# GNN kernel: edge counts summed on GpSimd during the adjacency loop, degrees formed as columns first

## The chip, the cores and the metric

The kernel is one program on one core of a Trainium2 chip. It is written directly for the five engines: TensorE (PE), VectorE (DVE), ScalarE (ACT), GpSimd (POOL) and SyncE (SP). Each engine has its own stream of instructions, and the streams wait for one another on semaphores. The metric is the device time of one execution, in microseconds; lower is better.

## The reference

A graph of 1250 nodes, each with 512 features, and 41250 directed edges, sorted by destination; every node also has its own loop once in the edge list. The work is a chain of four blocks with residual additions. What matters here is the first block, a graph convolution of three layers, and the third, which uses the same graph:

```python
loops = jnp.arange(n, dtype=edge_index.dtype)
src = jnp.concatenate([edge_index[0], loops])
dst = jnp.concatenate([edge_index[1], loops])
deg = jax.ops.segment_sum(jnp.ones_like(dst, dtype=x.dtype), dst, num_segments=n)
dis = jax.lax.rsqrt(jnp.maximum(deg, 1.0))
norm = (dis[src] * dis[dst])[:, None]
for l in range(W.shape[0]):
    h = x @ W[l]
    msg = h[src] * norm
    agg = jax.ops.segment_sum(msg, dst, num_segments=n) + b[l]
    x = jax.nn.relu(agg)
...
cnt = jax.ops.segment_sum(jnp.ones((src.shape[0],), x.dtype), dst, num_segments=n)
mean_agg = agg / jnp.maximum(cnt, 1.0)[:, None]
```

`deg` (edges into a node, plus one) scales the rows before and after each layer; `cnt` (edges into a node) is needed much later, as 1/cnt.

## The kernel before

**The adjacency table.** The kernel turns the edge list into a dense table `CTR`: for each of ten tiles t of 125 source nodes, 125 partitions (the source node in its tile) by 1250 columns (the destination node), holding the number of edges. It is built in 33 batches (`NBAT`) of 1250 edges. For each batch VectorE writes two one-hot tables in f16 (`onehots`, L1536 for the source in its tile, L1541 for source tile and destination slot; each is a TENSOR_TENSOR of two inputs in SBUF), TensorE multiplies them into a PSUM bank (L1052; L1034 opens the bank, L1027 adds the first column of the next batch and so ends the bank), and ScalarE copies 50 columns of all ten tiles into `CTR` (L722) at a place read from a register. ScalarE's copies are counted by the semaphore `placed`. Because edges are sorted by destination, batches fill the table from left to right; columns on the left are final long before the loop ends. Batch b's one-hots go to one of three buffers (`RING`), so VectorE may not start batch b before TensorE has finished batch b-3. In the loop ScalarE also sums rows of X and their squares (L731, L737) for the layer norm; GpSimd has nothing to do from 6.5 us on.

**The stage after the loop.** It is a chain through four engines:

- TensorE waits for all 33 copies (`placed`), then `degrees` (L1083) multiplies a table of ones (`WH`, 128 columns) with all of `CTR`: 3 column splits (500, 500, 250) by 10 tiles, 30 products. The result is the degree of every destination as a row, the same in all 128 partitions, in banks 0 to 2.
- VectorE copies the three pieces into `invc` (L1649, `deg_copied`), then adds the identity to the ten diagonal blocks of `CTR` (`self_loops`, L1644, `loops_ready`).
- TensorE turns the row into columns: ten products of one row of `invc` by a single 1 (L1094, `degcol_ready`), one column per tile, in bank 3.
- ScalarE takes the square root (L743), VectorE the reciprocal (L1653): `dis`. Then for each tile ScalarE writes `YH` = `XHAT`*`dis` rounded (L754) and VectorE the rest `YL` (L1668, `y_ready`), and TensorE starts the first aggregation (L1110: `YH` and `YL` of each tile times `CTR`, 12 groups of 20 products in each of three layers).

`XHAT`, the normalised input, is written by VectorE right behind its last one-hot (L1589, ten TENSOR_SCALARs). Later VectorE takes max(., 1) and the reciprocal of `invc` (L1676, L1677).

The order on every engine is the order in which the code is written; nothing is moved by a scheduler. A flag set during the loop chooses at run time between this path and a slow one for unusual edge lists; with these inputs the first one runs, and the slow path only costs branches. SyncE only starts transfers, of which none is in flight in this stage that anything here waits for.

Of the kernel before, what the change touches and what calls it, by code (L numbers as in the profile page):

```python
# [22 lines left out]
N = 1250  # L23
# [20 lines left out]
FLAG_AT = 5  # L44
SUMS_AT = 2
# [54 lines left out]
def build(nc, a, out):  # L100
    ctx = ExitStack()
    with ctx:
# [3 lines left out]
        def sem(name):  # L106
            return ctx.enter_context(nc.semaphore(name))
# [64 lines left out]
        XT = at("XTF", R_ZH, [128, NT * D])  # L172
        XTH = at("XTH", R_ZH, [128, FT, N], F32R)
# [45 lines left out]
        wbase, edge, offs, holds = carve(NG + 1), carve(NBAT), carve(NG), carve(2 * NG + NBAT)  # L219
# [84 lines left out]
        sp_ready, sp_exp, sp_one, sp_ln = sem("sp_ready"), sem("sp_exp"), sem("sp_one"), sem("sp_ln")  # L304
# [237 lines left out]
        def _(pool):  # L542
# [20 lines left out]

            pool.wait_ge(agg_ready, FT * len(SPLITS) * LAYERS)
# [132 lines left out]
        def _(act):  # L697
# [59 lines left out]
            act.wait_ge(deg_ready, len(SPLITS))  # L757
# [3 lines left out]
            act.wait_ge(sp_one, 1)  # L761
# [242 lines left out]
        def _(pe):  # L1004
# [75 lines left out]
            def degrees(unit, table):  # L1080
                for s, (c0, w) in enumerate(SPLITS):
                    for t in range(NT):
                        mm = nc.tensor.matmul(PS[:, s, 0:w], unit, table[0:NP, t, c0:c0 + w],  # L1083
                                              start=(t == 0), stop=(t == NT - 1))
                    mm.then_inc(deg_ready, 1)

            with pe.If(slow < 1):
                degrees(WH[0:NP, 0, 0:128], CTR)
            with pe.If(slow > 0):
                pe.wait_ge(counts_ready, 1)  # L1090
                degrees(ones[0:NP, :], CT)
# [29 lines left out]
            def gcn(exact):  # L1121
                n_agg = 0
                for l in range(LAYERS):
                    for s, (c0, w) in enumerate(SPLITS):
                        for f in range(FT):
                            if n_agg >= 6:
                                pe.wait_ge(zl_ready, n_agg - 5)
                            tile_wait = None
# [121 lines left out]
            pe.wait_ge(loops_ready, 2)  # L1250
# [219 lines left out]
        def _(dve):  # L1470
# [82 lines left out]
            def check_windows():  # L1553
# [5 lines left out]
                link(v.tensor_scalar(holds[0:1, 2 * NG + NBAT - 1:], wbase[0:1, NG - PER:NG - PER + 1], float(CW - BWIN - 1), None, ALU.is_le))  # L1559
# [35 lines left out]
            with dve.If(slow > 0):  # L1595
                SLOW0, SLOWK = 3, 7
# [597 lines left out]
```

## Time and profile before

| | us |
|---|---|
| median of 3 runs (lowest, highest) | 867.35 (866.24, 869.72) |
| the profiled execution | 867.76 |
| its span, first to last instruction | 865.8 |
| last copy into the table ends | 79.53 |
| the 30 degree products begin, end | 79.70, 88.04 |
| first product of the first aggregation | 93.18 |

| engine | busy us | share of the span |
|---|---|---|
| PE | 794.6 | 92% |
| DVE | 530.7 | 61% |
| ACT | 314.4 | 36% |
| POOL | 140.8 | 16% |

Times in rows are microseconds from the start of the span. "L1083" is line 1083 of the kernel printed above. In a row of a timeline the first number is the start, the second the length of the record; the names after the line are the operation and the tiles it writes and reads. "x30" says that 30 instructions are merged in the row, and brackets tell how long the engine had been idle and who ended that. One f32 product is recorded as two passes; so the ten products of L1094 are twenty records. Records of neighbouring instructions of one engine overlap a little, so the distance between starts is what an instruction costs there.

### The profile page before, as it was taken

The page shows a single profiled execution, that of the slowest core. Times are in us where ns is not written, and L with a number is a line of the kernel's source. Part 1 is how long each engine was busy: PE and PEld are TensorE (multiplying, and loading weights), DVE is VectorE, ACT ScalarE, POOL GpSimd, SP SyncE. Part 2 cuts the span into 40 slices and gives each one's busy share as a digit, 9 for nine tenths or more (in the row PEclk, how much of TensorE's full clock was granted, in tenths as well). Part 3 has the DMA queues.
Part 4 walks back from the last instruction along what each step waited for, and adds up shares of the span by engine and source line. Part 5 has one row for each costly group of instructions (what it writes and reads, how often), then busy time and mean ns, then how long its engine had stood idle before and what let it go on. Part 6 is the DMA issues. An engine that isn't in the chain of part 4 may idle for free.

```text
span 865.8 us, 13538 instructions
## 1 busy us (share of the span) xinstructions
PE 794.6 (92%) x3933; PEld 620.2 (72%) x3934; DVE 530.7 (61%) x949; ACT 314.4 (36%) x522; POOL 140.8 (16%) x186
## 2 busy tenths in 40 slices
PE   3899899999999989997999969987989999999983
PEld 1556788888888876676888847876867777777761
DVE  7777832421431587886024685897477878778751
ACT  1563512511431104533211313332245655556531
POOL 2000000000000300000000500212123443455321
PEclk9999899999999999998999978987989999999997
DMA  7400000000000010000102003002898959874632
GB/s 195 139 2 2 0 1 1 1 1 1 0 1 1 31 51 0 1 1 1 49 1 93 23 1 119 1 0 98 325 350 258 309 90 357 273 192 82 153 62 33
DMA packets 32291, 71.38 MB, mean 82 GB/s; under 512 B 4387, under 2 KB 4637, under 8 KB 32243
## 3 DMA queue, kind: packets, MB, share of 16 engines
q1 hardware_dynamic: 24480, 53.31, 17.7%
q0 software_dynamic: 6272, 14.68, 8.6%
q10 hardware_dynamic: 1491, 2.73, 0.9%
q8 instruction: 32, 0.52, 0.3%
q14 instruction: 16, 0.13, 0.0%
HBM read 96.53 MB, written 12.72 MB: 126 GB/s over the span
## 4 chain that ended last, share of the span: by engine, by line
PE 77%; DVE 15%; issue 3%; ACT 1%; DMA 1%; DVEq 1%; ACTq 0%; POOL 0%; POOLq 0%
PE PS L1110 22%; PE PS L1144 10%; PE PS L1363 9%; PE PS L1410 8%; PE PS L1242 5%; PE PS L1052 4%; PE PS L1357 4%; PE PS L1185 3%; PE PS L1395 3%; PE PS L1034 2%; PE PS L1341 1%; PE PS L1372 1%; PE PS L1083 1%; DVE stats L1892 1%; DVE XN L1480 1%
## 5 line engine op out<-in xcount | busy, mean ns | idle before, releaser
L1110 PE MATMUL PS<-CTR,YH 125*128 125x500 f32 (+1 forms) x480 | 164.1, 357 | 2.3 <-DVE YL L1668 2.3
L1110 PE MATMUL PS<-CTR,YL 125*128 125x500 f32 (+1 forms) x480 | 163.7, 356 | 0.0
L1110 PEld LDWEIGHTS PS<-CTR,YH 125*128 125x128 f32 x480 | 91.5, 191 | 15.5 <-DVE YL L1668 2.6
L1110 PEld LDWEIGHTS PS<-CTR,YL 125*128 125x128 f32 x480 | 91.6, 191 | 13.1
L1986 DVE TENSOR_TENSOR W1L<-WB,W1H 128x1152 fp32r<-128x1152 f32 x56 | 74.0, 1356 | 14.6 <-issue 7.7
L1410 PE MATMUL PS<-WB,YF 128*128 x168 | 78.6, 604 | 2.4 <-issue 1.7
L1695 DVE TENSOR_TENSOR ZL<-PS,ZH 128x500 fp32r<-128x500 f32 (+1 forms) x36 | 21.1, 592 | 90.2 <-ACT ZH L788 90.2
L1363 PE MATMUL PS<-W1H,XGH 128*128 128x384 f32 x168 | 73.5, 438 | 0.0
L961 ACT CAST W1H<-WB 128x1152 fp32r x56 | 64.2, 1151 | 15.9 <-issue 10.9
L1363 PE MATMUL PS<-W1L,XGH 128*128 128x384 f32 x168 | 57.4, 342 | 0.0
L1363 PE MATMUL PS<-W1H,XGL 128*128 128x384 f32 x168 | 56.9, 339 | 0.0
L671 POOL DMA_INDIRECT out<-YF,dest_i x28 | 48.2, 1722 | 34.5 <-ACT YF L936 18.7
L788 ACT CAST ZH<-PS 128x500 fp32r<-128x500 f32 (+1 forms) x36 | 18.1, 508 | 97.3 <-PE PS L1110 97.3
L1410 PEld LDWEIGHTS PS<-WB,YF 128*128 128x128 f32 x168 | 30.4, 194 | 30.8 <-issue 30.8
L1357 PE MATMUL PS<-WB,YF 128*128 x112 | 46.1, 494 | 2.3 <-DVE W1L L1986 2.3
L1144 PE MATMUL PS<-WL,ZH 128*125 128x512 f32 x120 | 47.3, 394 | 0.0
L1144 PE MATMUL PS<-WH,ZH 128*125 128x512 f32 x120 | 47.3, 394 | 0.0
L1144 PE MATMUL PS<-WH,ZL 128*125 128x512 f32 x120 | 47.2, 394 | 0.0
L565 POOL MEMSET FMASK<- 128x1 f32 x1 | 0.1, 99 | 282.6 <-PE PS L1110 282.6
L1052 PE MATMUL PS<-ET 125*128 125x120 f16 x330 | 44.0, 309 | 2.1 <-issue 2.1
L1706 DVE SCALAR_TENSOR_TENSOR tmp<-PS,dis,bias 125x512 f32<-125x512 f32 x30 | 22.5, 751 | 35.7 <-PE PS L1144 35.7
L1052 PEld LDWEIGHTS PS<-ET 125*128 125x128 f16 x330 | 30.4, 135 | 18.3 <-issue 17.4
(386 smaller groups left out, 1638.3 us busy)
## 6 DMA issues: line engine op xcount, KB each, us to landing
WB<-in_w SPq DMA_DIRECT2D x28, 1536.0 KB
WB<-in_w SPq DMA_DIRECT2D x28, 768.0 KB
WB<-in_b SPq DMA_DIRECT2D x28, 384.0 KB
X<-in_x SPq DMA_DIRECT2D x1, 2240.0 KB
xn_dram<-XN SPq DMA_DIRECT2D x1, 2240.0 KB
WNEXT<-in_W SPq DMA_DIRECT2D x2, 1024.0 KB, 9.7
SR<-in_sw SPq DMA_DIRECT2D x1, 1536.0 KB, 7.8
out<-X ACTq DMA_DIRECT2D x1, 1120.0 KB
```

The costliest lines, as they stand in the source:

```text
L671: pool.indirect_dma_start(out[:, :], bass.IndirectOffsetOnAxis(dest_i[:, k:k + 1], 0), yo[:, k, :], None, compute_op=ALU.add).then_inc(sca ...
L961: nc.scalar.copy(W1H[k][:, :, cols], raw[:, :, cols]).then_inc(w1_hi, 1)
L1052: mm = nc.tensor.matmul(windows(b)[:, :, place], oh_lo[b % RING][0:CHUNK, j, :, x], oh_key[b % RING][0:CHUNK, j, :, x].rearrange("p (t w) ...
L1110: mm = nc.tensor.matmul(dest, lhs, rhs, start=(t == 0 and h == 0), stop=(t == NT - 1 and h == 1))
L1144: mm = nc.tensor.matmul(PS[0:NP, 6 + n % 2, :], z[:, f, t * NP:(t + 1) * NP], w[:, f, :], start=(f == 0 and h == 0), stop=(f == FT - 1 and ...
L1185: mm = nc.tensor.matmul(PS[0:TILE[j], 3 + j, 0:RC], w[rows, k, cols], x, start=(k == tiles[0] and h == 0), stop=(k == 2 and h == 2))
L1242: mm = nc.tensor.matmul(PS[:, 4 + n % 4, 0:w], wt[:, f, fo * 128:(fo + 1) * 128], z[:, f, c0:c0 + w], start=(f == 0 and h == 0), stop=(f = ...
L1357: nc.tensor.matmul(PS[:, 2 * k + h, 0:INTER], xgf[:, k, :], WB[:, bass.ds(off + (FR * H2 + h * INTER), INTER)], start=True, stop=False)
L1363: mm = nc.tensor.matmul(PS[:, 2 * k + h, 0:INTER], x[:, k, f, :], wt[k][:, f, cols], start=False, stop=(f == FR - 1 and j == 2))
L1395: nc.tensor.matmul(PS[0:NP, bank, :], x[:, c, nodes], wt[:, c, :], start=(c == 0 and j == 0), stop=False)
L1410: mm = nc.tensor.matmul(PS[:, 6 + k, :], tt[:, k, j, :], WB[:, bass.ds(off + (O_W2 + j * D), D)], start=(j == 0), stop=(j == 2))
L1986: v.tensor_tensor(W1L[k][:, :, cols], raw[:, :, cols], f32(W1H[k][:, :, cols]), ALU.subtract).then_inc(w1_lo, 1)
```

## The change

GpSimd gets a new piece of work in the adjacency loop. In four ranges of columns it sums the ten tiles of `CTR` into one table `TOTAL` (125 x 1250, in a part of ZH that is free then), nine additions per range, each waiting for the one before: columns 0 to 499 once 15 copies are placed, 500 to 874 after 25, 875 to 999 after 28, 1000 to 1124 after 31. The last 125 columns are not summed.

TensorE then waits for all 36 additions and for all copies. It makes the degree *columns* first: for tiles 0 to 8 one product of a 125 x 125 block of `TOTAL` with a column of ones, and for tile 9 ten products, one per source tile of `CTR`: 19 single-column f32 products. After them come the row for the last 126 columns (ten products of 126 columns, bank 5, `deg_ready` 1), and the row for the rest from `TOTAL` (124, 500 and 500 columns, banks 5, 6, 7, `deg_ready` 2).

VectorE adds the identity to eight diagonal blocks as soon as the 36 additions are done, takes the reciprocal `dis`, waits for `deg_ready` 1 and adds the other two. The row is read (max with 1 included) behind the ten `YL` instructions; `deg_copied` is now awaited by the sixth aggregation group, which reuses bank 5. Four one-element comparisons join the checks of the edge list, so that an order of edges for which a range would not be final takes the slow path.

```diff
+RANGES = ((0, 500, 15), (500, 875, 25), (875, 1000, 28), (1000, 1125, 31))
+LAST0 = N - NP
+ROW0 = LAST0 - 1
...
+            for c0, c1, b in RANGES:
+                pool.wait_ge(placed, b)
+                for t in range(1, NT):
+                    before = CTR[0:NP, 0, c0:c1] if t == 1 else total[0:NP, c0:c1]
+                    if t > 1:
+                        pool.wait_ge(summed, added)
+                    pool.tensor_tensor(total[0:NP, c0:c1], f32(before), f32(CTR[0:NP, t, c0:c1]), ALU.add
+                                       ).then_inc(summed, 1)
+                    added += 1
...
-            def degrees(unit, table):
-                for s, (c0, w) in enumerate(SPLITS):
-                    for t in range(NT):
-                        mm = nc.tensor.matmul(PS[:, s, 0:w], unit, table[0:NP, t, c0:c0 + w],
-                                              start=(t == 0), stop=(t == NT - 1))
-                    mm.then_inc(deg_ready, 1)
-
+            def degrees(table, each, sums, last, unit):
+                for t in range(NT):
+                    for k in range(NT if t == NT - 1 else 1):
+                        lhs = table[0:NP, k, LAST0:N] if t == NT - 1 else each[0:NP, t * NP:(t + 1) * NP]
+                        mm = nc.tensor.matmul(PS[0:NP, 3, t:t + 1], lhs, ones[0:NP, 0:1], start=(k == 0),
+                                              stop=(t < NT - 1 or k == NT - 1))
+                mm.then_inc(degcol_ready, 1)
+                for k in range(NT):
+                    mm = nc.tensor.matmul(PS[:, 5, ROW0 - 1000:N - 1000], unit, last[0:NP, k, ROW0:N],
+                                          start=(k == 0), stop=(k == NT - 1))
+                mm.then_inc(deg_ready, 1)
+                for bank, c0, c1 in ((5, 1000, ROW0), (6, 500, 1000), (7, 0, 500)):
+                    mm = nc.tensor.matmul(PS[:, bank, 0:c1 - c0], unit, sums[0:NP, c0:c1], start=True, stop=True)
+                mm.then_inc(deg_ready, 1)
+
+            pe.wait_ge(summed, (NT - 1) * len(RANGES))
             with pe.If(slow < 1):
-                degrees(WH[0:NP, 0, 0:128], CTR)
+                degrees(f32(CTR), f32(total), total, CTR, WH[0:NP, 0, 0:128])
...
-            pe.wait_ge(deg_copied, 1)
-            for t in range(NT):
-                mm = nc.tensor.matmul(PS[0:NP, 3, t:t + 1], invc[0:1, t * NP:(t + 1) * NP], ones[0:1, 0:1],
-                                      start=True, stop=True)
-            mm.then_inc(degcol_ready, 1)
-            pe.wait_ge(loops_ready, 1)
+            pe.wait_ge(loops_ready, 2)
...
+                for k, (_, past, b) in enumerate(RANGES):
+                    v.tensor_scalar(holds[0:1, 2 * NG + NBAT + k:2 * NG + NBAT + k + 1], wbase[0:1, b * PER:b * PER + 1],
+                                    float(past - 1), None, ALU.is_ge)
...
-            for s, (c0, w) in enumerate(SPLITS):
-                dve.wait_ge(deg_ready, s + 1)
-                ins = v.tensor_copy(invc[:, c0:c0 + w], PS[:, s, 0:w])
-            ins.then_inc(deg_copied, 1)
-            self_loops(ALU.add, loops_ready)
+            dve.wait_ge(summed, (NT - 1) * len(RANGES))
+            self_loops(ALU.add, loops_ready, range(NT - 2))
             dve.wait_ge(sd_ready, 2)
             v.reciprocal(dis[0:NP, :], dis[0:NP, :]).then_inc(dis_ready, 1)
             dve.wait_ge(dis_ready, 1)
+            dve.wait_ge(deg_ready, 1)
+            self_loops(ALU.add, loops_ready, range(NT - 2, NT))
```

On TensorE, between the last batch of the loop and the first aggregation, the kernel before has these instructions (lines are its own; CT and its products belong to the slow path):

```order
L1087 COMPARE_AND_BRANCH [waits placed]
L1083 MATMUL PS<-CTR,WH 128x500 x20
L1083 MATMUL PS<-CTR,WH 128x250 x10
L1087 UNCONDITIONAL_BRANCH
...
L1094 MATMUL PS<-ones,invc 125x1 [waits deg_copied]
L1094 MATMUL PS<-ones,invc 125x1 x9
L1148 COMPARE_AND_BRANCH [waits loops_ready]
```

In the changed kernel the same place reads as follows (its lines are those of the new file):

```order
L1112 COMPARE_AND_BRANCH [waits summed,placed]
L1100 MATMUL PS<-ones,TOTAL 125x1 x9
L1100 MATMUL PS<-ones,CTR 125x1 x10
L1104 MATMUL PS<-CTR,WH 128x126 x10
L1108 MATMUL PS<-TOTAL,WH 128x124
L1108 MATMUL PS<-TOTAL,WH 128x500 x2
```

The 30 wide products are gone, the columns have moved to the front and no longer wait for VectorE's copy, and 13 products of the row follow them; the stage now opens with a wait for GpSimd's additions.

On GpSimd, between the constants and the next work (which waits for the end of all three layers), the changed kernel has:

```order
L565 AFFINE_SELECT below<-below 128x128
L576 TENSOR_TENSOR TOTAL<-CTR 125x500 [waits placed]
L576 TENSOR_TENSOR TOTAL<-TOTAL,CTR 125x500 [waits summed] x8
L576 TENSOR_TENSOR TOTAL<-CTR 125x375 [waits placed]
L576 TENSOR_TENSOR TOTAL<-TOTAL,CTR 125x375 [waits summed] x8
L576 TENSOR_TENSOR TOTAL<-CTR 125x125 [waits placed]
L576 TENSOR_TENSOR TOTAL<-TOTAL,CTR 125x125 [waits summed] x8
...
L581 MEMSET FMASK 128x1 [waits agg_ready]
```

All 36 additions are new (the last two rows stand twice, for ranges 3 and 4); before, the AFFINE_SELECT was followed directly by the MEMSET.

On VectorE, behind XHAT, the changed kernel has:

```order
L1672 COMPARE_AND_BRANCH [waits summed,const_done]
L1675 TENSOR_TENSOR CTR<-CTR,ident 125x125 x8
...
L1681 RECIPROCAL dis<-dis 125x10 [waits sd_ready]
L1672 COMPARE_AND_BRANCH [waits deg_ready,dis_ready]
L1675 TENSOR_TENSOR CTR<-CTR,ident 125x125 x2
...
L1698 SCALAR_TENSOR_TENSOR YL<-XHAT,dis,YH 125x512 [waits yh_ready,val_ready] x10
L1702 TENSOR_SCALAR invc<-PS 128x500 [waits deg_ready]
```

The copies out of PSUM have moved behind the ten YL instructions, and two of the ten self-loops now stand behind a wait for TensorE's ten products of 126 columns.

## Rows read from the trace of the kernel before

**Rows 1.** Page, chain of work that ended last: shares by engine.

```profile
PE 77%; DVE 15%; issue 3%; ACT 1%; DMA 1%; DVEq 1%; ACTq 0%; POOL 0%; POOLq 0%
```

**Rows 2.** Chain from 79 to 93.3 us: start, us, what.

```profile
79.70 8.34 PE PS L1083 x30
...
88.54 2.35 PE PS L1094 x20
...
92.38 0.76 DVE YL L1668
...
93.18 0.78 PE PS L1110
```

**Rows 3.** Groups of POOL by form: shapes, count, busy us, mean ns, idle.

```profile
L642 POOL TENSOR_TENSOR TL<-ST,TH 128x500 fp32r<-128x500 f32 x6 | 7.2, 1199 | 35.7 <-ACT TH L900 35.7
...
L642 POOL TENSOR_TENSOR TL<-ST,TH 128x250 fp32r<-128x250 f32 x3 | 2.1, 693 | 12.7 <-ACT TH L900 12.7
...
289.48 4.93 POOL L572 TENSOR_SCALAR_AFFINE_SELECT FMASK<-FMASK 15x1 f32<-15x1 f32 x15
```

**Rows 4.** Timeline of VectorE: batch 17's one-hots, XHAT, self-loops.

```profile
46.87 0.82 DVE L1536 TENSOR_TENSOR ET<-ET 125x1280 f16<-125x1280 f16 x1
47.60 0.78 DVE L1541 TENSOR_TENSOR ET<-ET 125x1200 f16<-125x1200 f16 x1
...
75.93 4.65 DVE L1589 TENSOR_SCALAR XHAT<-X,minus,rstd 125x512 f32<-125x512 f32 x10
...
88.40 2.08 DVE L1644 TENSOR_TENSOR CTR<-CTR,ident 125x125 fp32r<-125x125 f32 x10
```

**Rows 5.** Timeline of TensorE: the products just ahead of batches 20 and 21.

```profile
55.05 0.23 PE L1027 MATMUL PS<-ET 125*128 125x10 f16 x1
...
56.80 0.23 PE L1027 MATMUL PS<-ET 125*128 125x10 f16 x1
```

**Rows 6.** Timeline of ScalarE: the 15th, 25th and 33rd copy.

```profile
46.59 0.59 ACT L722 CAST CTR<-PS 125x500 f32 x1 [1.21 <-PE PS L1027]
...
65.40 0.59 ACT L722 CAST CTR<-PS 125x500 f32 x1 [0.47 <-PE PS L1027]
...
78.94 0.59 ACT L722 CAST CTR<-PS 125x500 f32 x1 [0.52 <-PE PS L1052]
```

**Rows 7.** Timelines of VectorE and GpSimd, three places where both read SBUF.

```profile
556.43 0.73 DVE L1922 SCALAR_TENSOR_TENSOR ST<-SG,SC,ST 128x500 f32<-128x500 f32 x1
...
584.49 1.07 POOL L642 TENSOR_TENSOR TL<-ST,TH 128x500 fp32r<-128x500 f32 x1 [2.03 <-ACT TH L900]
...
584.80 1.29 DVE L1922 SCALAR_TENSOR_TENSOR ST<-SG,SC,ST 128x500 f32<-128x500 f32 x1
...
301.02 0.69 DVE L1714 SCALAR_TENSOR_TENSOR X<-tmp,X 125x512 f32<-125x512 f32 x1
...
301.17 0.61 POOL L589 TENSOR_TENSOR W3S<-FFNR,W3S 107x12 fp32r<-107x12 f32 x1
...
752.22 1.56 POOL L652 COPY idx<-tok 128x1 int32 x1
...
752.40 2.63 DVE L1986 TENSOR_TENSOR W1L<-WB,W1H 128x1152 fp32r<-128x1152 f32 x2 [0.28 <-issue]
...
753.67 1.35 DVE L1986 TENSOR_TENSOR W1L<-WB,W1H 128x1152 fp32r<-128x1152 f32 x1
```

**Rows 8.** Timeline at the start: two equal VectorE casts, GpSimd beside the first.

```profile
4.45 1.22 DVE L1492 CAST ET<-ET 125x330 f32<-125x330 int32 x1 [4.32 <-DMA ET<-in_src]
...
4.96 0.52 POOL L553 MEMSET XTF<- 128x512 f32 x1
...
5.58 0.33 DVE L1493 CAST ET<-ET 125x330 f32<-125x330 int32 x1
```

**Rows 9.** Chain from 15 to 24 us: a one-element check.

```profile
19.41 0.07 DVE ET L1559
```

**Rows 10.** Windows in a run of f32 128-column products (L1117): busy us (count), clock.

```profile
322.00:324.00 2.00, 2.00 (x12) 2.00 (x12) 1.93 (x5) 0.00 (x0) 0.00 (x0) 0.54 0.06 22
```

More of the change, by code:

```diff
@@ L172, in build @@
         XT = at("XTF", R_ZH, [128, NT * D])
+        total = at("TOTAL", R_ZH + ROWB // 2, [128, N], F32R)
         XTH = at("XTH", R_ZH, [128, FT, N], F32R)
@@ L218, in build @@
         limit, weight, packed = carve(PER), carve(PER), carve(NG)
-        wbase, edge, offs, holds = carve(NG + 1), carve(NBAT), carve(NG), carve(2 * NG + NBAT)
+        wbase, edge, offs, holds = carve(NG + 1), carve(NBAT), carve(NG), carve(2 * NG + NBAT + len(RANGES))
         bad = sb("bad", [128, 4])
@@ L756, in _ @@
             act.wait_ge(zeroed, 16)
-            act.wait_ge(deg_ready, len(SPLITS))
+            act.wait_ge(deg_ready, 2)
             split_weight(0, WRAW[:, :, :], "w0", 16)
@@ L1127, in gcn @@
                                 pe.wait_ge(zl_ready, n_agg - 5)
+                            if n_agg == 5:
+                                pe.wait_ge(deg_copied, 1)
                             tile_wait = None
@@ L1248, in _ @@
             sage_linear([(f, s) for s, f in SF], hr_ready, hr_ps, sxt_ready)
-            pe.wait_ge(loops_ready, 2)
+            pe.wait_ge(loops_ready, 3)
             pe.wait_ge(y_ready, NT * (LAYERS + 1))
@@ L1558, in check_windows @@
                                 chain[0:1, 0, PER * OWN:NCH:PER * OWN], ALU.is_gt)
-                link(v.tensor_scalar(holds[0:1, 2 * NG + NBAT - 1:], wbase[0:1, NG - PER:NG - PER + 1], float(CW - BWIN - 1), None, ALU.is_le))
+                for k, (_, past, b) in enumerate(RANGES):
+                    v.tensor_scalar(holds[0:1, 2 * NG + NBAT + k:2 * NG + NBAT + k + 1], wbase[0:1, b * PER:b * PER + 1],
+                                    float(past - 1), None, ALU.is_ge)
+                link(v.tensor_scalar(holds[0:1, 2 * NG + NBAT - 1:2 * NG + NBAT], wbase[0:1, NG - PER:NG - PER + 1], float(CW - BWIN - 1), None, ALU.is_le))
                 link(v.tensor_reduce(bad[0:1, 3:4], holds[0:1, :], AX.X, ALU.min))
@@ L1633, in _, with self_loops @@
                         dve.wait_ge(slow_step, w * (SLOWK + NSG) + g + (SLOW0 + SLOWK + 1))
+                for t in range(1, NT):
+                    v.tensor_tensor(invc[0:NP, :], CT[0:NP, 0, 0:N] if t == 1 else invc[0:NP, :], CT[0:NP, t, 0:N], ALU.add
+                                    ).then_inc(slow_step, 1)
+                    dve.wait_ge(slow_step, SLOW0 + PASSES * (SLOWK + NSG) + t)
             v.memset(bad[:, 3:4], 0.0).then_inc(counts_ready, 1)
             dve.wait_ge(const_done, CONSTS)
-            def self_loops(op, signal):
+            def self_loops(op, signal, tiles=range(NT)):
                 for table, on in ((CTR, slow < 1), (CT, slow > 0)):
                     with dve.If(on):
-                        for t in range(NT):
+                        for t in tiles:
                             dest = table[0:NP, t, t * NP:(t + 1) * NP]
@@ L1669, in _ @@
                                        in1=f32(YH[0:NP, t, :]), op0=ALU.mult, op1=ALU.subtract).then_inc(y_ready, 1)
+            dve.wait_ge(deg_ready, 2)
+            for bank, (c0, w) in zip((7, 6, 5), SPLITS):
+                ins = v.tensor_scalar(invc[:, c0:c0 + w], PS[:, bank, 0:w], 1.0, None, ALU.max)
+            ins.then_inc(deg_copied, 1)
             split_weight(0, WRAW[:, :, :])
@@ L1673, in _ @@
             v.tensor_tensor(clampv[:, 1, :, :], clampv[:, 0, :, :], acts[:, :, 3:5], ALU.min).then_inc(sp_ready, 1)
-            dve.wait_ge(degcol_ready, 1)
-            link(v.tensor_scalar(invc[:, :], invc[:, :], 1.0, None, ALU.max))
+            dve.wait_ge(deg_copied, 1)
             link(v.reciprocal(invc[:, :], invc[:, :]))
             dve.wait_ge(sp_exp, 1)
-            v.tensor_scalar(clampv[:, 3, :, :], clampv[:, 2, :, :], 1.0, None, ALU.add).then_inc(sp_one, 1)
+            v.tensor_scalar(clampv[:, 3, :, :], clampv[:, 2, :, :], 1.0, None, ALU.add).then_inc(sp_ready, 1)
             dve.wait_ge(sp_ln, 1)
```

8 lines of the change are left out of this document (5 added, 3 removed).

## Prediction

> **What bounds the kernel now.** I read the page first: the chain that ended last is TensorE for 77% of the span and VectorE for 15%, GpSimd 0% [rows 1]. So a gap of TensorE in the first stages is paid in full, and whatever moves the first aggregation moves the end by as much, since everything behind it is the same work bound by the same engine. Next I read the chain from the last copy to the first aggregation. The last copy ends at 78.94 + 0.59 = 79.53 [rows 6]. Then come 8.34 us of wide products, VectorE's last copy, 2.35 us for the twenty passes of the columns, and 2.29 us (from 88.54 + 2.35 = 90.89 to 93.18) for root, reciprocal, YH and YL [rows 2]. That is 13.65 us, the only stretch the change can shorten. Last I looked at who is free in the loop: GpSimd has nothing, VectorE works 1.43 us a batch (two one-hots at distances of 0.73 and 0.70; the records are 0.82 and 0.78) [rows 4], and TensorE needs 1.75 us a batch [rows 5]. VectorE's slack is therefore about 0.33 us a batch. It decides this case.
>
> **What the change removes.** The 8.34 us of products leave the path, with VectorE's last copy (0.5 us to 88.54). If nothing else waited, TensorE would start the columns at 79.6.
>
> **GpSimd's additions by themselves.** The same operation, f32 with two inputs in SBUF, takes 1.20 us on 500 columns and 0.69 on 250 [rows 3], that is 2.0 ns a column and a fixed 0.19. So I take 0.95 for 375 columns and 0.43 for 125. Each waits for the one before. In the fifteen selects that also wait each for its predecessor, the distance is 4.93 / 15 = 0.33 [rows 3], against about 0.2 for the work; I take 0.13 for the hand-over. Alone, the ranges would take 9 x 1.33 = 12.0, 9 x 1.08 = 9.7 and twice 9 x 0.56 = 5.0 us. From the 15th copy (47.2) the first ends at 59.2; from the 25th (66.0) [rows 6] the second ends at 75.7, the third at 80.7 and the fourth at 85.7. Even undisturbed, TensorE is held until 85.7, not 79.6.
>
> **They will not be undisturbed.** Three places in the trace show that the two engines exclude each other when both read SBUF [rows 7]. The VectorE instruction of 0.73 us took 1.29 when it began 0.31 us into a GpSimd addition: 0.56 longer, until 585.36, which is 0.20 before the GpSimd record ends (585.56). In the other direction, a GpSimd addition of twelve columns, worth 0.2 us, took 0.61: it began in earnest about 0.13 before the end of the VectorE record (301.71). And a GpSimd copy at 752.22 ended at 753.78, between two VectorE additions that follow each other directly (the second starts at 753.67): GpSimd is let in between two instructions. So I let them take turns. In a turn VectorE holds 0.67 (0.80 less 0.13) and GpSimd 1.20 - 0.19 = 1.01 at 500 columns, 0.76 at 375, 0.24 at 125; turns are 1.68, 1.43 and 0.91 us. GpSimd is back 0.32 us after it lets go, before VectorE's one-hot is over, so the turns are strict.
>
> Range 1: 9 x 1.68 = 15.1 us, to 62.5. A batch needs two one-hots, so VectorE now makes one in 3.4 us instead of 1.43. Its 17th (counted from 0) was half done at 47.6; the 21st is done at 63.1, and TensorE starts it at 63.2 instead of 56.9 [rows 5]: 6.3 late. TensorE then runs at its own pace again, and the 25th copy comes at 66.0 + 6.2 = 72.2. Range 2: 9 x 1.43 = 12.9, to 85.2. Batches 27 to 30 come every 2.9 us. Range 3 begins at once beside the last two batches; the last one-hot ends near 88.7, batch 32 starts some 11 us late, and the 33rd copy lands near 91. XHAT follows on VectorE. Its ten take 0.465 each for 512 elements [rows 4], more than the two-input form reaches, and such one-input instructions collide too: a cast of 0.33 took 1.22, until 5.67, with GpSimd's memset up to 5.48 beside it [rows 8]. Turns there are about 0.42 + 0.24 = 0.66. Range 3 ends near 92.4, and range 4, part in turns of 0.66 and part alone at 0.56, near 98.0. A bound from below is that one-hots (22.6 us from 47.2) and holds of GpSimd (9 x 2.25 = 20.3 with two of 0.24) can't overlap: no end before 90. A bound from above comes with the rival of starvation.
>
> The Trainium skill, "SBUF — State Buffer", section "Who interferes with whom", says that a VectorE instruction with two SBUF inputs contends with a GpSimd instruction that reads SBUF, and that the first holds the pair of ports for its whole instruction. The trace agrees on the exclusion but lets the other in 0.13 to 0.20 us before a record ends. Held for the whole record, a turn of range 1 would be 2.0 instead of 1.68, and the end of range 4 some 5 us later.
>
> **The columns.** 19 products are 38 passes. A pass costs 2.35 / 20 = 0.117 before [rows 2]; there TensorE had been busy with wide products. Now it comes from batches that wait on VectorE and from a gap of some 7 us. At a granted clock of 0.54, near the lower level of 1.2 GHz, 12 passes of 128 columns take 2.0 us, 0.165 each [rows 10]. So 4.5 to 6.3 us; I take 5.4, in between, for a single column is the narrower case. This replaces the 2.35.
>
> **Behind the columns.** Root and reciprocal are as before. VectorE then waits for the ten products of 126 columns, 10 x (0.117 to 0.165) = 1.2 to 1.7 us behind the columns, and adds two self-loops at 2.08 / 10 = 0.21 each [rows 4], with some branches; YL takes 0.76 [rows 2]. The first aggregation starts 2.6 to 3.3 after the columns, I take 2.9, instead of 2.29. Queued behind that wait are the YLs, which TensorE awaits. The three products from `TOTAL` lie under it.
>
> **What costs nothing.** The reading of the row, max and reciprocal stand behind the YLs; the first that needs them is the sixth aggregation group, a hundred wide products later: cover is ample (without it, three reads of some 0.7 us would be on the path). The four checks of one element stand in VectorE's chain ahead of the loop: 4 x 0.07 = 0.3 us [rows 9], on the path. The two products of 500 columns ahead of the aggregation may keep the clock up; YL paces the first group anyway, so I count 0, with 0.5 in the range.
>
> **Sum.** 98.0 + 0.3 + 5.4 + 2.9 = 106.6 against 93.18: 13.4 us later. The profiled execution took 867.76, so it would take 881.2; it lies 0.4 above the median of the runs, so 880.8. With GpSimd's quickest addition (1.07 [rows 7]) range 4 ends at 95.7, with a slow 1.3 at 100; with both ends of the columns the forecast's own range is 876 to 885.
>
> **Rivals.**
>
> *No exclusion for f16 one-hots.* The rows show it for f32 only, and one-hots read mostly repeated elements. Then the sum is 85.7 + 0.3 + 5.4 + 2.9 = 94.3, 1.1 late: 868.5, and 866.5 with the quicker ends. Nothing in the profile supports this except that the case isn't shown. 0.18.
>
> *Starvation.* GpSimd gets in only when VectorE idles. For it: at the start VectorE's cast was kept out over three GpSimd instructions, not one [rows 8]; against it, the copy let in at 753.6. VectorE's slack of 0.33 x 16 batches holds five additions of range 1 up to 75.7; TensorE's loop hardly suffers. XHAT runs to 80.6; then four of 1.33, nine of 1.08 and eighteen of 0.56 are left, 25.1 us: 105.7. 105.7 + 0.3 + 5.4 + 2.9 = 114.3: 21 late, 888.5. 0.12.
>
> *The other side: the additions keep pace.* If GpSimd adds counts so much faster than in its rows that all are done with the last copy, the columns start at 79.6 and the aggregation at 79.6 + 0.3 + 5.4 + 2.9 = 88.2, 5.0 early: 862.4, and 860 with quick columns. It decides from an addition of 500 columns near 0.9, of 125 near 0.2. No row is near. 0.07.
>
> **Chances.** The forecast holds 0.63. An interval measurement of this kernel tells about 0.5%, 4.3 us, from no change. Faster 0.07 (the last rival), same 0.18 (the first), slower 0.75. The range reaches down to the rival without exclusion and up to starvation: 866 to 889.
>
> **What would show it.** Right: one-hots of VectorE of 1.5 us and more between the 15th copy and 62; batches 18 to 21 of TensorE 3.4 us apart; GpSimd additions of up to 1.9 us; the 33rd copy near 91; `TOTAL` complete near 98; 38 passes in 5.4. Wrong: one-hots that stay at 0.82 and a last copy at 79.8 (then the first rival, or starvation if GpSimd's additions are stretched instead), or additions well under 1.2 us.

## The result, and the profile of the changed kernel

The changed kernel takes 885.08 us in the median (883.92 to 887.18, four runs) against 866.86 for the kernel before (866.24 to 869.72, four runs): ratio 1.021, 95% interval 1.019 to 1.023. It is slower, as forecast; the forecast was 880.8 us, so 4.3 us too short: inside the stated range of 866 to 889, but just past the 876 to 885 that the prediction gave the forecast itself. The profiled execution took 884.98 us with a span of 883.2; before it was 867.76 with 865.8. So 17.4 us of span are to be found.

The page first: busy time of two engines, and the chain of work that ended last (answers to [rows 1]). Lines from here on are those of the changed kernel: L576 is the addition on GpSimd, L1558 and L1563 are the one-hots, L738 the copy into `CTR`, L1100 the columns, L1130 the aggregation.

```profile
PE 800.2 (91%) x3934; PEld 620.9 (70%) x3935; DVE 546.7 (62%) x952; ACT 313.8 (36%) x522; POOL 175.4 (20%) x222
...
PE 73%; DVE 16%; issue 4%; POOL 3%; ACT 2%; DMA 1%; DVEq 1%; ACTq 0%; SPq 0%; POOLq 0%
```

GpSimd, at 0% of the chain before, now has 3% of it, and TensorE fell from 77% to 73% though its busy time grew. Something of GpSimd's stands in TensorE's way. The timeline of GpSimd shows all 36 additions (start, us, operation, shapes; nine per range, the first apart from the other eight):

```profile
47.48 2.05 POOL L576 TENSOR_TENSOR TOTAL<-CTR 125x500 fp32r<-125x500 f32 x1 [40.97 <-ACT CTR L738]
...
49.61 13.33 POOL L576 TENSOR_TENSOR TOTAL<-TOTAL,CTR 125x500 fp32r<-125x500 f32 x8
...
72.95 1.19 POOL L576 TENSOR_TENSOR TOTAL<-CTR 125x375 fp32r<-125x375 f32 x1 [10.01 <-ACT CTR L738]
74.22 11.39 POOL L576 TENSOR_TENSOR TOTAL<-TOTAL,CTR 125x375 fp32r<-125x375 f32 x8
85.58 0.99 POOL L576 TENSOR_TENSOR TOTAL<-CTR 125x125 fp32r<-125x125 f32 x1
86.64 5.70 POOL L576 TENSOR_TENSOR TOTAL<-TOTAL,CTR 125x125 fp32r<-125x125 f32 x8
92.31 0.58 POOL L576 TENSOR_TENSOR TOTAL<-CTR 125x125 fp32r<-125x125 f32 x1
92.97 4.19 POOL L576 TENSOR_TENSOR TOTAL<-TOTAL,CTR 125x125 fp32r<-125x125 f32 x8
```

Range 1 ends at 62.94, range 2 at 85.61, range 3 at 92.34, range 4 at 97.16. Range 2 waits 10 us for its columns to be placed; ranges 3 and 4 start the moment the one before is done, so from range 2 on GpSimd never catches up. In range 1 the distance is 13.33 / 8 = 1.67 us. VectorE at the same time, beside range 1 and beside range 2 (answers to [rows 4], where the one-hots were 0.82 and 0.78):

```profile
50.14 1.82 DVE L1563 TENSOR_TENSOR ET<-ET 125x1200 f16<-125x1200 f16 x1
51.88 1.69 DVE L1558 TENSOR_TENSOR ET<-ET 125x1280 f16<-125x1280 f16 x1
...
74.75 1.55 DVE L1563 TENSOR_TENSOR ET<-ET 125x1200 f16<-125x1200 f16 x1
76.23 1.47 DVE L1558 TENSOR_TENSOR ET<-ET 125x1280 f16<-125x1280 f16 x1
```

Every one-hot beside these two ranges contains one of GpSimd's additions. A batch, two one-hots, takes 1.61 + 1.74 = 3.35 us of VectorE by the chain of waits, where TensorE would need 1.75. TensorE waits for it; these are the products just ahead of its batches 19 and 20, 3.26 us apart (answers to [rows 5]; the bracket tells how long TensorE had been idle and who ended that):

```profile
55.75 0.20 PE L1043 MATMUL PS<-ET 125*128 125x10 f16 x1 [1.28 <-DVE ET L1563]
...
59.01 0.20 PE L1043 MATMUL PS<-ET 125*128 125x10 f16 x1 [1.24 <-DVE ET L1563]
```

Batch 20 stood at 55.05 before [rows 5], so at this point the loop is 4.0 us late.

The 33rd copy into the table, which ended at 79.53 before [rows 6], now starts at 91.20 (0.59 us). The stage behind the loop, in the chain of waits (answers to [rows 2]):

```profile
97.44 8.13 PE PS L1100 x38
105.58 2.25 PE PS L1104 x10
...
108.43 0.74 DVE YL L1698
...
109.22 20.81 PE PS L1130 x82
```

The first aggregation starts at 109.22 instead of 93.18: 16.0 of the 17.4 us. The other 1.4 come later and are taken up below.

### The profile page after: what moved, and what is told of

The parts are those of the page before. It is cut to its first block, busy times and chain, and to the rows that moved or that the text cites. A ratio compares the mean times of both kernels' runs of the same rounds, so it can differ in the third digit from the quotient of the medians.

```text
span 883.2 us, 13583 instructions
## 1 busy us (share of the span) xinstructions
PE 800.2 (91%) x3934; PEld 620.9 (70%) x3935; DVE 546.7 (62%) x952; ACT 313.8 (36%) x522; POOL 175.4 (20%) x222
## 3 DMA queue, kind: packets, MB, share of 16 engines
q1 hardware_dynamic: 24480, 53.31, 17.4%
## 4 chain that ended last, share of the span: by engine, by line
PE 73%; DVE 16%; issue 4%; POOL 3%; ACT 2%; DMA 1%; DVEq 1%; ACTq 0%; SPq 0%; POOLq 0%
PE PS L1130 21%; PE PS L1166 9%; PE PS L1385 9%; PE PS L1432 8%; PE PS L1264 5%; PE PS L1379 4%; PE PS L1207 3%; PE PS L1417 3%; POOL TOTAL L576 3%; PE PS L1068 2%; DVE ET L1563 1%; DVE ET L1558 1%; PE PS L1137 1%; PE PS L1363 1%; PE PS L1394 1%
## 5 line engine op out<-in xcount | busy, mean ns | idle before, releaser
L1130 PE MATMUL PS<-CTR,YH 125*128 125x500 f32 (+1 forms) x480 | 163.8, 356 | 0.3 <-DVE YL L1698 0.3
L1130 PE MATMUL PS<-CTR,YL 125*128 125x500 f32 (+1 forms) x480 | 163.2, 355 | 0.0
L1130 PEld LDWEIGHTS PS<-CTR,YH 125*128 125x128 f32 x480 | 91.2, 190 | 14.5 <-DVE YL L1698 1.7
L1130 PEld LDWEIGHTS PS<-CTR,YL 125*128 125x128 f32 x480 | 91.4, 190 | 12.8
L1068 PE MATMUL PS<-ET 125*128 125x120 f16 x330 | 46.5, 307 | 3.4 <-issue 3.4
L1068 PEld LDWEIGHTS PS<-ET 125*128 125x128 f16 x330 | 28.5, 129 | 22.5 <-issue 20.9
```

The lines of the kernel that those rows point to most:

```text
L1068: mm = nc.tensor.matmul(windows(b)[:, :, place], oh_lo[b % RING][0:CHUNK, j, :, x], oh_key[b % RING][0:CHUNK, j, :, x].rearrange("p (t w) ...
L1130: mm = nc.tensor.matmul(dest, lhs, rhs, start=(t == 0 and h == 0), stop=(t == NT - 1 and h == 1))
```

## The experiments

The theory to be tested is that of the prediction: a GpSimd addition and a VectorE instruction that reads two inputs from SBUF exclude each other, so that the loop runs at the pace of both in turn, and the sums are late even so. Against it stood: that one-hots in f16 are not touched; that only GpSimd's slowness counts, not the collision; that what follows the sums costs as much as they do. Medians of the kernel before, run beside the experiments, lay between 866.58 and 867.48. Experiments 7 and 8 ask whether a part of the idea pays.

**1. The work on GpSimd without its reads.** The 36 instructions stay, at the same places and with the same waits, but write a constant; they read nothing.

```diff
-                    pool.tensor_tensor(total[0:NP, c0:c1], f32(before), f32(CTR[0:NP, t, c0:c1]), ALU.add
-                                       ).then_inc(summed, 1)
+                    pool.memset(f32(total[0:NP, c0:c1]), 1.0).then_inc(summed, 1)
```

> The changed kernel with each of the 36 additions on GpSimd replaced by a memset of the same columns of TOTAL, with the same waits; nothing on GpSimd reads SBUF in the loop, and the degrees are wrong by that. Theory (GpSimd's reading excludes VectorE's two-input one-hots): one-hots stay at 0.82 and 0.78 us, the 33rd copy ends near 79.9, TOTAL is there by 80.5; then the columns as measured, 8.1 us, and 3.7 to the first aggregation: about 92.2 against 109.2, so some 17 us less than the changed kernel, 868. Rival (any GpSimd instruction, or the waits and semaphores themselves, disturb the loop): one-hots stretched by 0.3 to 0.5 us each beside the memsets, the 33rd copy at 84 or later, 872 and more.

It took 867.97 us, ratio 1.002 (1.000 to 1.004). VectorE's timeline in this kernel, then GpSimd's, then the chain of waits:

```profile
66.73 0.82 DVE L1557 TENSOR_TENSOR ET<-ET 125x1280 f16<-125x1280 f16 x1
67.46 0.78 DVE L1562 TENSOR_TENSOR ET<-ET 125x1200 f16<-125x1200 f16 x1
...
76.21 4.66 DVE L1613 TENSOR_SCALAR XHAT<-X,minus,rstd 125x512 f32<-125x512 f32 x10
```

```profile
66.31 4.16 POOL L576 MEMSET TOTAL<- 125x375 f32 x9 [13.72 <-ACT CTR L737]
71.94 2.28 POOL L576 MEMSET TOTAL<- 125x125 f32 x9 [1.47 <-ACT CTR L737]
77.02 3.99 POOL L576 MEMSET TOTAL<- 125x125 f32 x9 [2.80 <-ACT CTR L737]
```

```profile
81.28 8.13 PE PS L1099 x38
89.41 2.25 PE PS L1103 x10
...
93.06 46.95 PE PS L1129 x231
```

One-hots are back at 0.82 and 0.78 although GpSimd writes beside them, and the last copy ends at 79.23 + 0.59 = 79.82. So it is GpSimd's reading that stretches them. The second reading is the more important one: with sums that are practically free, the first aggregation starts at 93.06, which is where the kernel before starts it. Against the changed kernel, TensorE starts its columns 97.44 - 81.28 = 16.2 us earlier, and what stands behind, up to the first aggregation, has the same length (11.8 us both times). All of the loss at the first aggregation is the sums, and all that the new order of the degrees can bring, as written, is nothing.

**2. The additions without the collision.** All 36 wait until the last copy is placed.

```diff
-                pool.wait_ge(placed, b)
+                pool.wait_ge(placed, NBAT)
```

> The changed kernel with all 36 additions held back until the 33rd copy. Theory: the loop is undisturbed, the last copy ends near 79.9, and the additions alone take 9 x 1.33, 9 x 1.08 and 18 x 0.56, 31.8 us (a little more beside XHAT), to 112; first aggregation near 124, 15 us later than in the changed kernel: 900. Rival (the additions are slow by themselves in this table, 1.67 us each at 500 columns): 15.0 + 12.7 + 11 = 39 us, to 119, 907.

One run: 897.47 us (900 expected). The loop is undisturbed (last copy at 79.76). GpSimd's timeline, and the groups of its instructions by form (busy us, mean ns of one):

```profile
79.83 1.90 POOL L576 TENSOR_TENSOR TOTAL<-CTR 125x500 fp32r<-125x500 f32 x1 [73.32 <-ACT CTR L738]
81.82 9.78 POOL L576 TENSOR_TENSOR TOTAL<-TOTAL,CTR 125x500 fp32r<-125x500 f32 x8
```

```profile
L576 POOL TENSOR_TENSOR TOTAL<-TOTAL,CTR 125x500 fp32r<-125x500 f32 x8 | 9.2, 1154 | 0.6
L576 POOL TENSOR_TENSOR TOTAL<-TOTAL,CTR 125x375 fp32r<-125x375 f32 x8 | 7.3, 912 | 0.6
L576 POOL TENSOR_TENSOR TOTAL<-TOTAL,CTR 125x125 fp32r<-125x125 f32 x16 | 6.8, 427 | 1.3
```

Alone an addition is 1.15, 0.91 and 0.43 us, at distances of 1.22, 0.98 and 0.50, and all 36 take 29.3 us. The prediction had 1.20, 0.95 and 0.43 with 0.13 between them; the hand-over is 0.07. In the changed kernel the same forms measure 1.60, 1.36 and 0.55. So both sides pay: an addition 0.44 us more, a one-hot 0.9 to 1.0 us more. And it is better to collide than to wait: the first aggregation starts at 121.19 here, 12.0 later than in the changed kernel.

**3. One input instead of two on GpSimd.** The additions become copies of the same columns. The degrees, and the routing behind them, then differ; the one run took 831.54 us with 1161 instructions fewer in its trace than the changed kernel has (12422 against 13583), so only the loop is read from it, not its time.

```diff
-                    pool.tensor_tensor(total[0:NP, c0:c1], f32(before), f32(CTR[0:NP, t, c0:c1]), ALU.add
-                                       ).then_inc(summed, 1)
+                    pool.tensor_copy(total[0:NP, c0:c1], f32(CTR[0:NP, t, c0:c1])).then_inc(summed, 1)
```

> The changed kernel with each addition replaced by a copy of one tile of CTR to TOTAL: one input instead of two on GpSimd (the degrees are wrong by that). Theory (exclusion is by whole instructions as soon as GpSimd reads SBUF): one-hots are stretched by the length of a copy less 0.2 us, about 0.4 us at 500 columns if a copy takes 0.6; 33rd copy near 83, 875. Rival (only two-input instructions on both sides collide): one-hots at 0.82, copy at 79.9, 868.

VectorE beside range 1:

```profile
48.54 1.22 DVE L1557 TENSOR_TENSOR ET<-ET 125x1280 f16<-125x1280 f16 x1
49.69 1.18 DVE L1562 TENSOR_TENSOR ET<-ET 125x1200 f16<-125x1200 f16 x1
```

The one-hots still collide, and are 0.40 us longer instead of 0.9 to 1.0. The last copy ends at 83.28, against 79.82 in experiment 1 and 91.79 in the changed kernel: 3.5 us late instead of 12.0. So one input that GpSimd reads is enough to exclude. A copy is shorter than an addition (at 125 columns, alone, 0.29 us against 0.43), and the price follows the length: beside additions of 500, 375 and 125 columns the first one-hot of a pair takes 1.69, 1.47 and 1.06 us.

**4. Are the columns slow because TensorE comes from a wait?** Eighteen f32 products of 128 columns that nobody reads fill TensorE's wait for the sums.

```diff
+            for _ in range(18):
+                nc.tensor.matmul(PS[:, 4, 0:128], ones[:, :], ident[:, :], start=True, stop=True)
             pe.wait_ge(summed, (NT - 1) * len(RANGES))
```

> The changed kernel with 18 f32 products of 128 columns (36 passes) of constants on TensorE while it waits for GpSimd, into a bank nobody reads. Theory A (the columns are slow because TensorE comes out of a gap at the lower clock): the 38 passes take 0.117 each, 4.5 instead of 8.1 us, the ten products of 126 columns 1.2 instead of 2.2: 4.6 us less, 880.5. Theory B (a pass that loads 125 x 125 f32 weights costs 0.21 us at any clock): columns stay at 8.1 us, 885.

It took 881.11 us, ratio 1.018 (1.014 to 1.022). The chain of waits, and three windows (busy us and count of TensorE's products, its weight loads, VectorE, ScalarE and GpSimd, then the granted clock, DMA share, GB/s):

```profile
91.86 5.64 PE PS L1112 x36
97.51 4.16 PE PS L1100 x38
101.67 2.22 PE PS L1104 x10
```

```profile
97.50:99.50 2.00, 2.00 (x21) 2.00 (x20) 1.58 (x8) 0.00 (x0) 0.00 (x0) 1.00 0.00 0
99.50:101.60 2.10, 2.10 (x21) 2.10 (x21) 0.00 (x0) 0.00 (x0) 0.00 (x0) 0.99 0.00 0
101.60:103.80 2.20, 2.20 (x12) 2.20 (x12) 0.22 (x1) 1.76 (x4) 0.00 (x0) 0.50 0.03 7
```

Behind the filler the 38 passes take 4.16 us, 0.109 each, at a granted clock of 1.00; in the changed kernel they take 8.13, 0.214 each. The ratio is 1.95, close to that of the two levels of 2.4 and 1.2 GHz. And the clock falls right behind the columns: the ten products of 126 columns run at 0.50 and take 2.22 us, as without the filler. So the first aggregation comes 3.9 us earlier (105.28). The median is 4.0 lower, but the four runs lie between 878.73 and 886.33, so it is the trace that shows the gain. One caution for reading: the changed kernel's windows over 97.5 to 105.5 print a clock of 1.00, with 10 or 11 passes in 2 us where this kernel has 21. There the printed level is not that of the work: the trace has no record of the clock until a rise at 112.8 us, and 1.00 is printed for want of one. The pace of the passes tells the level.

**5. Half the passes.** `TOTAL` and `CTR` hold small whole numbers; in the format fp32r a product is one pass instead of two. The kernel makes two equal columns per tile and ScalarE reads every second.

```diff
-                        mm = nc.tensor.matmul(PS[0:NP, 3, t:t + 1], lhs, ones[0:NP, 0:1], start=(k == 0),
+                        mm = nc.tensor.matmul(PS[0:NP, 3, 2 * t:2 * t + 2], lhs, unit[0:NP, 0:2], start=(k == 0),
...
-                degrees(f32(CTR), f32(total), total, CTR, WH[0:NP, 0, 0:128])
+                degrees(CTR, total, total, CTR, WH[0:NP, 0, 0:128])
```

> The changed kernel with the 19 column products in fp32r with two equal columns of ones, one pass each instead of two. Theory (a pass at the lower clock costs 0.21 us, whatever it is): 19 x 0.21 = 4.1 instead of 8.1 us, 881. Rival (a pass costs by its columns, or the fp32r form reloads at the same total): 885.

It took 880.57 us, ratio 1.017 (1.016 to 1.019). From the chain of waits:

```profile
97.44 4.14 PE PS L1100 x19
```

The passes are half as many and each 0.218 us, against 0.214 before: two columns in the new format cost what one does in the old. Format and width changed together, but the changed kernel tells the same: its 38 passes of one column start 0.21 us apart, and the ten of 126 columns behind them 0.21 to 0.22. The first aggregation starts at 105.23, 4.0 earlier.

**6. Columns first at its best.** The diffs of experiments 1 and 5 together: free sums (a constant is written, nothing is summed) and 19 passes.

> e1_memset (memsets in place of the additions, degrees wrong by that) together with the one-pass columns of e7_one_pass: what columns first could give at best if the sums were free. Theory: TOTAL ready at 81.0, 4.1 us of columns, 3.7 to the first aggregation: 89.0 against 93.2 in the kernel before, 863. Rival (later waits on VectorE take the gain back): 866 to 867.

It took 863.76 us, ratio 0.9956 (0.9938 to 0.9975). From the chain of waits:

```profile
81.27 4.14 PE PS L1099 x19
```

The first aggregation starts at 89.06, 4.1 before that of the kernel before. This is a bound for the idea, not a kernel: about 0.4% if the sums cost nothing and the columns are single-pass.

**7. Less to sum.** On the kernel before: GpSimd sums columns 0 to 499 alone, nine additions. The row is made as before, except that one product from `TOTAL` replaces the ten of its first piece; the columns stay where they were. In `e5_one_range` the additions follow one another from the 15th copy on, in `e6_spaced` addition t waits for two more copies than t-1. The core, and the line that differs between the two:

```diff
+                    if s == 0 and table is CTR:
+                        nc.tensor.matmul(PS[:, 0, 0:w], unit, total[0:NP, 0:w], start=True, stop=True
+                                         ).then_inc(deg_ready, 1)
+                        continue
...
-                pool.wait_ge(placed, 15)
+                pool.wait_ge(placed, 15 + 2 * (t - 1))
```

> The kernel before, with only columns 0 to 499 summed on GpSimd, nine additions at once after the 15th copy; the row of the first 500 columns is then one product of TOTAL instead of ten of CTR, all else as before (row first, columns by L1094). Theory: nine turns of 1.68 us make TensorE's loop 6.3 us late (33rd copy near 86), nine wide products at the lower clock of 0.42 us are saved, 3.7, less some 1.3 because the raised clock comes later: 870 to 871 against 866.9. Rival (VectorE's lead makes up for the turns): 864.

> As e5_one_range, but addition t waits for copy 15 + 2(t - 1), one in every second batch. Theory: a hold of 1.01 us per two batches is covered by VectorE's slack of 0.33 us a batch and its lead of two batches; demand is 9.1 us, slack from the 15th copy to the last one-hot 5.3 plus a lead of 2: the loop ends 0 to 2 us late, the nine products save 2.4 to 3.7: 864.5 to 867. Rival (slack doesn't help, each hold costs TensorE its full length): as slow as e5_one_range.

They took 872.88 us, ratio 1.008 (1.005 to 1.010), and 869.86 us, ratio 1.005 (1.003 to 1.006). In the spaced one, an addition and the one-hot beside it:

```profile
50.83 1.76 POOL L570 TENSOR_TENSOR TOTAL<-TOTAL,CTR 125x500 fp32r<-125x500 f32 x1 [1.45 <-ACT CTR L731]
```

```profile
50.67 0.81 DVE L1550 TENSOR_TENSOR ET<-ET 125x1280 f16<-125x1280 f16 x1
51.41 1.82 DVE L1555 TENSOR_TENSOR ET<-ET 125x1200 f16<-125x1200 f16 x1
```

and its chain behind the loop:

```profile
82.28 0.60 ACT CTR L731
...
83.13 0.78 PE PS L1093
83.91 5.95 PE PS L1097 x20
```

The addition is issued beside one one-hot, which keeps its 0.81; the next one carries it whole, 1.82. Nine additions at 1.0 us each are more than VectorE's slack over the spaced stretch, which covers 5.7 us of the 9: the last copy is 3.3 us late (82.88). Back to back it is 6.7 late (86.24; 6.3 was expected). What the sums bring: the row takes 6.7 us (83.13 to 89.86) instead of 8.34 [rows 2]. Nine products fewer save 1.6 us and no more, although before the first ones were 0.42 us apart, because what is left now begins at that slow pace: of the wide products saved most are the later ones, at 0.22, and seven of the 250-column products behind them are now 0.21 apart instead of 0.12. I had expected 2.4 us or more. So the price is greater than the gain either way: spacing the additions halves the price, but the 864.5 to 867 us that I expected of it are missed.

**8. Summing on VectorE itself.** On the kernel before: seven reductions of VectorE, each over ten tiles of 125 columns, as soon as these are final; no work on GpSimd. Two products from `TOTAL` and ten of 376 columns make the row.

```diff
+                for j, (n, at_b) in enumerate(REDUCE):
+                    if b == at_b:
+                        dve.wait_ge(placed, n)
+                        v.tensor_reduce(total[0:NP, j * NP:(j + 1) * NP],
+                                        f32(CTR[0:NP, :, j * NP:(j + 1) * NP]).rearrange("p t w -> p w t"),
+                                        AX.X, ALU.add).then_inc(summed, 1)
```

> The kernel before (row first, columns by L1094) with seven tensor_reduce on VectorE in the loop, each summing 125 finished columns over the ten tiles into TOTAL, three or four batches apart (seven checks of one element added); the row is then two products of TOTAL (500, 374 columns) and ten of CTR (376 columns). GpSimd does nothing. Theory: a reduce of 1250 elements takes 1.35 us against a slack of 0.33 us per batch plus VectorE's idle waits, so the loop ends 0 to 1 us later; the row takes 4.0 us instead of 8.3; the columns, now at the lower clock, 4.3 instead of 2.35; checks 0.5: 0.7 to 2.3 us less than before, 864.5 to 866. Rival (the reduces make TensorE wait as the turns did): the loop ends 3 us late or more, 868 and up.

It took 872.34 us, ratio 1.006 (1.004 to 1.009). VectorE's timeline, then the chain:

```profile
31.47 2.35 DVE L1587 TENSOR_REDUCE TOTAL<-CTR 125x125 fp32r<-125x1250 f32 x1
```

```profile
88.57 0.60 ACT CTR L726
...
89.33 1.09 PE PS L1088 x2
90.42 3.15 PE PS L1092 x10
```

The row is down to 4.24 us from 8.34. But a reduction takes 2.35 us, not the 1.35 that I had counted on. Seven of them are 16.4 us; VectorE's slack covers 6.8 of these, and the last copy is 9.6 late (89.17). The columns, for which I had counted 4.3 us at the lower clock, took 2.35 as in the kernel before. The first aggregation starts at 98.85. It is again the loop that pays, as the rival said.

None of the runs whose time can be compared beats the kernel before, except the bound in experiment 6, which leaves the sums out.

## Why the prediction was right, and where its sizes were off

**The additions by themselves** were a little quicker than predicted (experiment 2: distance 1.22 against 1.33 at 500 columns, 0.50 against 0.56 at 125), the hand-over 0.07 and not 0.13. **The exclusion** held as put: turns of 1.67 us in range 1 (predicted 1.68) and 11.39 / 8 = 1.42 in range 2 (1.43), and experiment 1 takes it away by taking GpSimd's reads away. That the turn fits to 0.01 us is in part luck, for its two terms were each some 0.05 off, in opposite directions: one-hots follow one another at 0.73 and 0.70 us, on average 0.715 and not 0.67, which leaves 1.67 - 0.715 = 0.96 us for an addition of 500 columns and not 1.01 (an estimate from these distances). Range 1 ended at 62.94 (62.5), range 2 at 85.61 (85.2), the last copy at 91.79 (near 91). The rival without exclusion is dead by the one-hots of 1.69 and 1.82; starvation is dead since GpSimd got its turn in every one-hot; that the additions keep pace is dead by their 1.15 us even alone.

The Trainium skill, "SBUF — State Buffer", section "Who interferes with whom", has it that a VectorE instruction with two SBUF inputs contends with a GpSimd instruction that reads SBUF but not with one that only writes. Experiments 1 and 3 and the changed kernel agree: one-hots of 0.82 beside writes, 1.22 beside copies, 1.69 beside additions. That the pair is held for the whole instruction, which the prediction draws on too, stands there in the line on VectorE's two-port modes; for the one-hots no row here shows it, since a turn is 1.67 us and not the 1.95 of whole records.

**Ranges 3 and 4.** Range 3 ended at 92.34 (92.4), but `TOTAL` was complete at 97.16 where 98.3 (98.0 and the checks) was put. Beside one-hots the additions of 125 columns started 0.95 us apart (0.91 predicted), beside XHAT 0.58 on average (0.66), and alone 0.51 (0.56); range 4 has only the last two kinds. XHAT, which reads one input, is slowed by them too, as the prediction put it, but by less: its ten took 5.63 us instead of 4.65 [rows 4].

```profile
89.26 5.63 DVE L1614 TENSOR_SCALAR XHAT<-X,minus,rstd 125x512 f32<-125x512 f32 x10
```

TensorE began the columns at 97.44, 0.9 before the forecast.

**The columns** are the term that was mis-sized most: 8.13 us against 5.4. The step that failed is the sentence that a pass lies between 0.117 and 0.165 and that "a single column is the narrower case". A narrower product is no quicker: what a pass costs here is not its one column. With two columns it takes the same (0.218, experiment 5), and TensorE's weight loads are busy for the whole of the windows over the columns (2.00 of 2.00 us, experiment 4). At the upper level it takes 0.109 (experiment 4), and the lower level doubles it to 0.214. The lower end, 0.117, was sound for the upper level: the passes of L1094 [rows 2] start 0.109 apart, just as those of experiment 4 do, although they load a single row of weights instead of 125. What was misread is the upper end, [rows 10]. It divides 2.0 us by a count of 12, but a window counts every record that reaches into it, and these records last up to 0.42 us, longer than the distance between them; besides, the clock was back at the upper level for the last 0.2 us. By their starts the same 128-column passes are 0.213 us apart at the lower level and 0.112 at the upper one, and 38 times 0.213 would have been 8.1. The Trainium skill, "TensorE: Matmul & The Clock Gate", section "LDWEIGHTS (loading the stationary operand)", makes a weight load of P columns take P/1.2 ns; an estimate from that is 104 ns for 125. The trace has 109 at the upper level, but 210 at the lower one.

**Behind the columns:** 109.22 - 105.57 = 3.65 us against 2.9. The ten products of 126 columns take 2.25, not up to 1.7, for the same reason (the misread upper end), and the two self-loops wait for them. VectorE's timeline (the bracket: idle 1.89 us, until TensorE's L1104):

```profile
108.02 0.49 DVE L1675 TENSOR_TENSOR CTR<-CTR,ident 125x125 fp32r<-125x125 f32 x2 [1.89 <-PE PS L1104]
```

These three add up to -0.9 + 2.7 + 0.75 = +2.6 us at the first aggregation (109.22 against 106.6); that the sums were early hid a third of what the columns were late.

**What costs nothing:** the row's reading behind the YLs was indeed covered, the first aggregation took 48.00 us where it had taken 48.56, and 0.22 us (46.81 against 46.59 for the 15th copy) is what the checks cost, 0.3 predicted.

**The other 1.4 us** were not in the prediction. The lead of 15.5 us holds through three layers; then 44 passes of filler products that keep TensorE busy take longer. TensorE's timeline in the changed kernel:

```profile
335.35 8.10 PE L1137 MATMUL PS<-ident,ones 128*128 128x128 f32 x44 [2.96 <-ACT sd L716]
```

and in the kernel before:

```profile
319.87 6.80 PE L1117 MATMUL PS<-ident,ones 128*128 128x128 f32 x44 [2.97 <-ACT sd L700]
```

By the trace's record of the clock, its lower level lasts for 6.2 us of that stretch after, and for 3.4 before; two windows, first the changed kernel's, then that of the kernel before:

```profile
339.30:341.30 2.00, 2.00 (x12) 2.00 (x11) 1.73 (x6) 0.00 (x0) 0.00 (x0) 0.50 0.00 0
```

```profile
324.00:326.00 2.00, 2.00 (x20) 2.00 (x20) 1.73 (x8) 0.00 (x0) 0.00 (x0) 1.00 0.00 0
```

Both windows begin about 4 us into the passes. The longer stretch does not look like a cost of GpSimd's additions, nor of the later start as such: `e1_memset`, which starts its aggregation as early as the kernel before, has the long form too, and `e7_one_pass`, which starts it 12 us later, the short one. From the start of the first layer's linear products to the first write of `FTT` behind this stretch it is 186.3 us in eight of the ten kernels and 187.4 in these two. From there to the end, with the same instructions in all of them, it is 536.0 to 541.7 us:

| kernel | first aggregation | from `FTT` to the end | span |
|---|---|---|---|
| before | 93.18 | 537.8 | 865.8 |
| after | 109.22 | 538.6 | 883.2 |
| `e1_memset` | 93.06 | 538.5 | 866.9 |
| `e2_late` | 121.19 | 540.3 | 895.7 |
| `e3_warm` | 105.28 | 538.2 | 877.8 |
| `e5_one_range` | 98.22 | 539.9 | 872.4 |
| `e6_spaced` | 95.01 | 537.2 | 866.7 |
| `e7_one_pass` | 105.23 | 536.0 | 875.7 |
| `e8_free_one_pass` | 89.06 | 541.7 | 865.1 |
| `e9_reduce` | 98.85 | 536.3 | 869.9 |

With the 2.6 us at the first aggregation this is 4.0 us of span, and the profiled execution came 3.8 above the forecast for it (884.98 against 881.2; what lies outside the span is 0.2 less than before).

From the table: an edit in the first 100 us of this kernel moves its end by its own amount, give or take 3 us. But each row is a single execution, and executions of one and the same kernel differ as much: the ten runs of experiment 6 lie between 861.41 and 866.93 us, and the profiled one is the slowest of them. Its span is only 0.7 below that of the kernel before where its stage saves 4.1, while the medians are 3.7 apart. So the table can't tell what belongs to a kernel and what to the execution, and this holds for the 1.4 us too. What sets the scatter stays open; the moments at which the clock changes differ between the traces, but no run here varies them alone.

## What to carry to other kernels

An idle engine is no free engine: before work goes to GpSimd, look at which VectorE instructions run at that time, and where these read two inputs from SBUF, as the one-hots do, count each GpSimd instruction that reads SBUF as added to them, with VectorE's slack against TensorE as all that there is to spend. An addition of ten tiles on GpSimd costs 1.0 us of VectorE per 500 columns and tile, and the TensorE product it saves costs 0.22 at the upper clock and 0.42 at the lower one; summing is what TensorE does cheaply. A pass over one column costs as much as a pass over 126 (0.21 to 0.22 us at the lower clock), so to save time count the passes and look at the level of the clock, not at the columns.

## What the runs showed of the hardware that I had not expected

- The two engines alternate strictly, one instruction each, in all of range 1 and 2, and the one that waits gets in before the record of the other ends: with whole records a turn would be 0.8 + 1.15 = 1.95 us, and it is 1.67. An addition issued beside a running one-hot leaves that one-hot alone and is carried by the next.
- GpSimd's constant writes of 125 columns took 0.25 us each beside the one-hots and 0.44 beside XHAT (2.28 and 3.99 us for nine, experiment 1), while XHAT kept its 4.66 us. XHAT has one SBUF input, the one-hots two: going by the place, it is the one-input instruction that holds GpSimd's writes up. Beside additions, which read, XHAT pays as well: 5.63 us.
- A stretch of single-column products, with TensorE busy by the records the whole time, was followed by the lower clock: 1.00 and 0.99 over the columns, 0.50 right behind (experiment 4). Why it fell there, no run here separates.
- A VectorE reduction over the tiles, 1250 f32 elements read with a stride of one tile, takes 2.35 us, 1.9 ns an element; XHAT's 512 elements take 0.465, 0.9 ns each.
